# A Mamba state scan: ScalarE's scaled copy of a turned tile comes half a state later, and TensorE turns the blocks of a state in another order

## What is computed

```python
delta = softplus(dt @ dt_w + dt_b)
def step(h, inputs):
    d_t, x_t, B_t, C_t = inputs
    dA = exp(d_t[..., None] * A)
    h = dA * h + (d_t * x_t)[..., None] * B_t[:, None, :]
    y = einsum('bds,bs->bd', h, C_t)
    return (h, y)
y = ys.transpose(1, 0, 2) + xi * D
y = y * silu(z)
return x + y @ out_proj
```

## Time and profile before

| | us |
|---|---|
| three runs | 573.67, 576.09, 575.18 (median 575.18) |
| the profiled execution | 575.25 |
| its span, first to last instruction | 573.5 |
| TensorE busy | 486.3 (85%) |
| VectorE busy | 462.5 (81%) |
| GpSimd busy | 387.0 (67%) |
| ScalarE busy | 371.7 (65%) |

### The profile page before, as it was taken

How to read it: one execution, slowest core, us unless ns; L and a number is a source line. 1 busy time by engine, 2 the same in 40 slices (tenths; PEclk the granted TensorE clock), 3 DMA queues, 4 the chain that set the end, 5 groups by cost and what they waited for, 6 DMA issues and landing times.

```text
span 573.5 us, 7946 instructions
## 1 busy us (share of the span) xinstructions
PE 486.3 (85%) x2777; PEld 340.7 (59%) x2777; DVE 462.5 (81%) x531; ACT 371.7 (65%) x650; POOL 387.0 (67%) x235
## 2 busy tenths in 40 slices
PE   8968999879868999998689999896797758789992
PEld 6424765455557675655575666465786546678651
DVE  4779989968899888879997888699989989951512
ACT  3766677667875766698858676888558759821210
POOL 5049978756798877759986777589959979510001
PEclk9978999955989999979999999799999979999997
DMA  9331111110111111111111111101211391039004
GB/s 290 107 113 37 38 37 38 39 39 37 34 40 38 37 39 38 39 37 38 38 38 38 38 37 38 39 2 37 75 37 38 110 405 45 2 87 345 0 1 151
DMA packets 17919, 38.88 MB, mean 68 GB/s; under 512 B 1665, under 2 KB 10497, under 8 KB 17874
## 3 DMA queue, kind: packets, MB, share of 16 engines
q1 hardware_dynamic: 17874, 38.32, 19.6%
HBM read 36.08 MB, written 2.23 MB: 67 GB/s over the span
## 4 chain that ended last, share of the span: by engine, by line
PE 47%; DVE 26%; issue 12%; ACT 10%; POOL 2%; DVEq 0%; ACTq 0%; POOLq 0%
DVE scanmem L1724 16%; PE hT L837 9%; PE pp L542 6%; PE pp L566 6%; PE yacc L600 4%; DVE yTd L1744 4%; PE pp L629 4%; PE pp L592 2%; ACT dA L1257 2%; PE dA L802 2%; POOL scanmem L1399 2%; PE pp L578 2%; ACT hc L1267 2%; PE pp L701 1%; PE pp L773 1%
## 5 line engine op out<-in xcount | busy, mean ns | idle before, releaser
L1399 POOL TENSOR_TENSOR scanmem<-par,scanmem 128x1024 f32<-128x1024 f32 x128 | 300.4, 2366 | 87.9 <-ACT carry L1282 41.6
L1257 ACT ACTIVATE dA<-par,Aneg 128x512 f32<-128x512 f32 x256 | 171.1, 690 | 45.2 <-DVE scanmem L1724 43.3
L837 PE MATMUL hT<-con,scanmem 128*128 128x128 f32 x1024 | 153.1, 290 | 43.2 <-DVE yTd L1744 21.3
L837 PEld LDWEIGHTS hT<-con,scanmem 128*128 128x128 f32 x1024 | 121.4, 148 | 100.0 <-issue 35.3
L1724 DVE TENSOR_TENSOR_SCAN scanmem<-dA,scanmem 128x512 f32<-128x512 f32 x128 | 150.3, 1207 | 22.3 <-ACT dA L1257 21.7
L1724 DVE TENSOR_TENSOR_SCAN scanmem<-dA,carry,scanmem 128x512 f32<-128x512 f32 x128 | 157.1, 1267 | 11.8 <-ACT dA L1257 11.5
L1267 ACT ACTIVATE hc<-hT,CTs 128x512 f32<-128x512 f32 x128 | 87.4, 683 | 75.4 <-PE hT L837 75.1
L600 PE MATMUL yacc<-con,hc 128*128 128x128 f32 x512 | 78.8, 294 | 11.2 <-ACT hc L1267 10.9
L600 PEld LDWEIGHTS yacc<-con,hc 128*128 128x128 f32 x512 | 62.9, 151 | 17.6 <-ACT hc L1267 13.7
L1744 DVE SCALAR_TENSOR_TENSOR yTd<-hT,CTs,yTd 128x512 f32<-128x512 f32 x85 | 62.1, 730 | 12.4 <-PE hT L837 12.0
L542 PE MATMUL pp<-xnT,wi 128*128 128x512 f32 x120 | 61.2, 640 | 4.9 <-ACT xnT L1036 3.2
(11 more groups left out here) (195 smaller groups left out, 507.6 us busy)
## 6 DMA issues: line engine op xcount, KB each, us to landing
scanmem<-brow SPq DMA_DIRECT2D x32, 512.0 KB, 3.7
par<-in SPq DMA_DIRECT2D x1, 4096.0 KB, 16.7
scanmem<-in SPq DMA_DIRECT2D x1, 4096.0 KB, 13.9
xt<-in SPq DMA_DIRECT2D x4, 512.0 KB, 6.7
wi<-in SPq DMA_DIRECT2D x2, 1024.0 KB, 7.0
out<-par SPq DMA_DIRECT2D x4, 512.0 KB, 4.1
aw<-in SPq DMA_DIRECT2D x5, 256.0 KB, 6.6
xr<-in SPq DMA_DIRECT2D x1, 1024.0 KB, 9.1
```

Source lines behind the costliest of these rows:

```text
L837: last = nc.tensor.transpose(hT[:, i % 2, m * P:(m + 1) * P], hb[:, n % RING, m, i * P:(i + 1) * P], ident)
L1257: A(dA[:, m % 2, :], delta(c)[:, m, :], ACT.Exp, scale=Aneg[:, m * NS + s:m * NS + s + 1]).then_inc(da_ready, 1)
L1399: nc.gpsimd.tensor_tensor(hb[:, n % RING, ms, :], dx(c)[:, ms, :], Bb[:, row:row + 1, :].to_broadcast([P, 2, T]), ALU.mult).then_inc(bx_re ...
```

## The change

- ScalarE's scaled copies move: in state n it copies block 2 of state n-2 behind exp 1, and block 0 of state n-1 behind exp 3. The carry is saved behind the first of the two.
- TensorE in state n: block 1 of state n-1, jobs h = 2n, block 0, block 3, `reduce` of block 2 of state n-2, block 2, `reduce` of block 0, jobs h = 2n+1. After the last scan: blocks 1, 0, 3, `reduce` of block 2 of state 62, block 2, then both reductions of state 63.
- VectorE multiplies the first bank of `yacc` with the gate in state 0 of a chunk and the second in state 1.
- In the last chunk jobs O go from h 3 and 5 to 4 and 6, and the first attention job from 6 to 7.

```diff
-LAST_EPILOGUE = {1: [("Y", 1)], 2: [("Y", 3)], 3: [("O", 0)], 5: [("O", 1)], 17: [("R", 0)], 19: [("R", 1)]}
-ATT = [6, 8, 8, 10, 12, 14, 15, 16, 17, 20, 22, 23, 24, 27]
+LAST_EPILOGUE = {1: [("Y", 1)], 2: [("Y", 3)], 4: [("O", 0)], 6: [("O", 1)], 17: [("R", 0)], 19: [("R", 1)]}
+ATT = [7, 8, 8, 10, 12, 14, 15, 16, 17, 20, 22, 23, 24, 27]
...
+TURNED = (1, 0, 3, 2)
+def turned(n, i):
+    return NT * n + TURNED.index(i) + 1
...
@@ TensorE, transposes @@
-                if i == 0:
+                if i == TURNED[0]:
                     pe.wait_ge(scan_done, CT * (n + 1))
...
@@ TensorE, one state @@
                     if n:
-                        transposes(n - 1, 0)
                         transposes(n - 1, 1)
                     for job in BESIDE[2 * n]:
                         run(job)
                     if n:
+                        transposes(n - 1, 0)
+                        transposes(n - 1, 3)
+                    if n >= 2:
+                        reduce(n - 2, 2)
+                    if n:
                         transposes(n - 1, 2)
-                        transposes(n - 1, 3)
                         reduce(n - 1, 0)
-                        reduce(n - 1, 2)
...
             n = NCH * NS
-            for i in range(NT):
-                transposes(n - 1, i)
+            transposes(n - 1, 1)
+            transposes(n - 1, 0)
+            transposes(n - 1, 3)
+            reduce(n - 2, 2)
+            transposes(n - 1, 2)
             reduce(n - 1, 0)
             reduce(n - 1, 2)
...
@@ ScalarE, one state @@
                     exp_step(n, 0)
                     exp_step(n, 1)
+                    if n >= 2:
+                        mul_step(n - 2, 2)
                     if n:
-                        mul_step(n - 1, 0)
+                        carry_step(n - 1)
                     for job in to_read(2 * n):
                         read(job)
                     exp_step(n, 2)
                     exp_step(n, 3)
                     if n:
-                        mul_step(n - 1, 2)
+                        mul_step(n - 1, 0)
                         pool_mul_step(n - 1)
-                        carry_step(n - 1)
...
@@ VectorE @@
-                    if s == 0 and c:
-                        gate_even(c - 1)
+                    if s < 2 and c:
+                        gate_even(c - 1, 2 * s)
```

17 lines of the change are left out of this document (9 added, 8 removed).

## The result

The changed kernel took 565.66 us in the median of four runs (565.45 to 567.58), the kernel before 575.42 (573.67 to 576.09): a ratio of 0.9841, 95% interval 0.9814 to 0.9867, 9.8 us faster. The profiled execution took 565.45 us, its span is 563.7 us against 573.5.

What follows compares the result with a forecast made beforehand. No engine is full: waits between engines bound the kernel, chiefly ScalarE's copy waiting for TensorE's turned block and delaying exps. 4.6 + 1.2 + 1.0 - 0.2 - 0.6 = 6.0 us, from 575.25 to 569.2; 8-in-10 range 562.5 to 574.5.

Steps and rivals of the forecast that it cites:

- ScalarE's copy at D: Copy behind exp 1 in the D and Z stretches: no longer delays the read of D; 4.6 us, bounds 0 and 8.7.
- rival C: First chunk's half-clock piece: TensorE's clock comes back sooner as stops around XT and D shorten; 564.5 us, chance 0.08.
- The stretches of V, X and O: States where TensorE sets the pace: nothing won; 185.5 to 240 was to change by under 1 us.
- rival D: I to O stretch: room by weight loads' share gives the entry part its upper bound, 6.3 us; 564.2 us, chance 0.04.
- The entry at state 2: Job I's entry: turned rows read about 1.2 us earlier, TensorE takes part back; 0.4 us in each of three chunks.
- The term for the new waits: Block 2 waits for block 0's copy; hidden by VectorE's scans where no job stands, shows in the softmax state: -0.2 us.
- rival B: New waits move a 10 us half-clock piece into the stretch where TensorE is full, in two chunks: 579 us, chance 0.12.
- The gate products: States 0 and 1 of a chunk: VectorE does the same work in the two states together, 0 us.
- O in the last chunk: Last chunk, O one half-state later: block 1 comes ahead of O; 1.0 us, bounds 0 and 2.04.
- The softmax state: Last chunk: a block's turn also waits for ScalarE, and block 1 of the next state behind it; -0.2 us.
- The end: Behind the last scan: one more reduction on TensorE makes O later; -0.6 us, bounds -1.2 and 0.
- Rivals A and E: A: TensorE takes the gain back, about 573.6, chance 0.15; E: the wait only moves, time stays at 575, chance 0.08.

Runs made afterwards that it cites:

- e7: The changed kernel with block 2's reduction of state 62 ahead of everything behind the last scan and D terms of the last bank behind the turns: 563.33 us, ratio 0.9777.
- e11: The changed kernel with e7's end, jobs behind both blocks in the first chunk and later states 0 to 3, and e9's products: 562.1 us, ratio 0.9771.
- e8: The changed kernel with five tiny VectorE instructions written as SCALAR_TENSOR_TENSOR: 566.41 us, ratio 0.9854 to the kernel before.
- e9: The changed kernel with three unread products between blocks 0 and 3 in the seven states without jobs: 567.76 us, ratio 0.9854 to the kernel before.

## Why the prediction was right, and where it was not

Faster, and inside the range: 565.7 us against 569.2 (562.5 to 574.5). By its steps:

**ScalarE's copy at D: right, and sized right in two chunks of three; the clock did the rest.** Exp 2 came 1.73 and 1.27 us earlier in the second and third chunks, where 1.77 and 1.31 were forecast, but 0.79 instead of 1.77 in the first, because I had let D end at the same place, and counted from the state's first scan it came 0.95 us later there. The three D and Z stretches gained 7.3 us where 4.6 was forecast. At equal half clock they gain 1.3 to 1.8 in the second chunk and, against 24.53 and 24.32 us in two kernels of the series with 10.2 us (e7, e11), 2.1 to 2.3 in the third. In the first, half clock of 7.5, 14.4 and 16.8 us (e7, e8, the change) went with 24.17, 25.72 and 26.70 us, about 0.27 us for each: of its 3.20 us, 5.7 x 0.27 = 1.5 are the clock (an estimate from these rows) and 1.7 the order. That is 5.1 to 5.8 us for the order; the other 2 are the half clock that fell away in the first and third chunks, less what came in the second. That is rival C in part, which I had at 0.08 for the first chunk alone; it is luck, since another execution of the same program has its half clock elsewhere.

**Two signs missed.** No scan in a state 10 was to wait over 1.7 us: 2.01, 2.02 and 2.14 us in the three chunks, 2.90, 2.90 and 3.32 before. In the second VectorE too reached that scan earlier, so that the wait fell by 0.88 us and exp 2's start by 1.73; the start was the number to forecast. And ScalarE's wait at the scaled copy was to fall below 40 us: it fell to 42.8.

**The stretches of V, X and O: right.** 44.01 to 44.07 and 43.63 to 43.59 us, clock 1.00. No kernel of the series took less, and two took 2.4 to 2.9 us more; the entries gained 1.25 to 1.39 us each, not rival D's 2.11. So the share of matmuls (42.69 of 44.07 us, 97%) was the better guide to what a new order could win here than that of the weight loads (28.92 us, 66%), and what the Trainium skill ("Perfetto Trace Analysis", "Identifying the Most-Contended Engine") would have made of this stretch did not come. That no kernel could be faster there isn't shown.

**The entry at state 2: mis-sized.** 1.39, 1.25 and 1.37 us where 0.4 each was forecast. The first half of the term was too small: 1.2 us was to be won, and in the second chunk the read came 2.02 us earlier and state 2 got 2.02 us shorter (8.54 to 6.52), because the 1.35 us which the copy had waited went too. What TensorE takes back, 0.8 us, was right: state 3 got 0.77 us longer (5.94 to 6.71), and in the third chunk it was 2.14 and 0.76. The jobs behind both blocks win 0.6 more.

**States 0 and 1: the step that failed.** I had them at 0; they lost 2.80 us, all with a piece of 3.4 us at half clock in each of three, which the kernel before hasn't. Without half clock the same states took 14.43 and 13.94 us in the experiments, as before, so neither the gate products nor the new order costs time there. The term for the new waits had them hidden by VectorE's scans where no job stands: the waits were, the clock was not in the term. In 1.0 to 1 TensorE's stops at VectorE's sums grew from 2.3 to 3.7 us; that these stops place the half clock is not shown, and e9, which filled them, moved it to other stretches. This is the effect of rival B in small, at another place than its own: the V stretch kept a clock of 1.00. 3.14 to 15 lost 1.60 us in the same way (11.13 us without half clock, 12.83 with 3.9, 15.94 with 10.5).

**The gate products, 0: right only in company.** Alone they cost 7.8 us; the deferred reduction is what makes them free.

**O in the last chunk: 1.0 forecast, 1.5 measured**, of which the rest of the change takes 0.5 in these states, so that 1.0 us is left, as forecast.

**The softmax state: wrong sign.** -0.2 us forecast, 1.15 won. VectorE and GpSimd of the changed kernel, then of the kernel before:

```profile
454.50 1.43 DVE L1589 TENSOR_TENSOR st<-st 128x1 f32<-128x1 f32 x1
```

```profile
453.56 2.35 POOL L1414 TENSOR_TENSOR scanmem<-par,scanmem 128x1024 f32<-128x1024 f32 x1
```

```profile
464.68 2.16 DVE L1575 TENSOR_TENSOR st<-st 128x1 f32<-128x1 f32 x1
```

```profile
462.14 4.68 POOL L1399 TENSOR_TENSOR scanmem<-par,scanmem 128x1024 f32<-128x1024 f32 x2
```

The operation on one element ends with GpSimd's instruction, which now happened to end earlier: 0.73 us of it. That is luck. I had taken every VectorE duration as fixed.

**The end: 0.6 forecast, 1.05 measured** on the path to O; the tail as a whole got 0.56 us shorter, because its half clock fell from 10.9 to 5.0 us.

**Rivals A and E fall.** TensorE did not take back two thirds of the gain at D, since 5.1 to 5.8 us of it came by the order. And exp 0 did not wait in place of exp 2: block 0's copy in state 10 of the second chunk waited for nothing, and in all of 1.10 to 12 ScalarE's scaled copies waited 1.8 us, 3.6 before.

So of the 3.8 us beyond the forecast, the entries and the softmax state bring 4.2 and the D and Z stretches and the tail 3.9, the most of it by the clock, against 4.4 us of new half clock in states 0 and 1 and in 3.14 to 15. The total was closer than its parts.
